# The router of a mixture of experts, merged into the stage of the shared expert

## What is computed

```python
g_s = silu(einsum('td,edf->etf', xf, Wg_s))
u_s = einsum('td,edf->etf', xf, Wu_s)
shared_out = einsum('etf,efd->td', g_s * u_s, Wd_s)      # F = 1536
logits = xf @ W_router + expert_bias                     # 625 x 8
top_vals, top_idx = jax.lax.top_k(logits, 2)
rw = softmax(top_vals, axis=-1)
...
routed_out = einsum('etd,te->td', out_e, combine)
x = x + shared_out + routed_out                          # xf is the layernorm of x
```

## Time and profile before

| what | us |
|---|---|
| device time, median of 3 runs | 2313.23 (2312.05 to 2313.57) |
| the profiled execution: its own time | 2312.01 |
| the profiled execution: span from its first to its last instruction | 2310.2 |
| PE, PEld, DVE, ACT, POOL busy | 2071.9, 1954.6, 1318.2, 888.6, 94.1 |
| the last four phases begin at about | 1450.6, 1469.6, 1520.0, 1718.2 |

### The profile page before, as it was taken

One profiled execution on the slowest core, in us unless ns is written; L12 is line 12 of the kernel. 1 busy time (PEld: TensorE's weight loads), 2 busy tenths in 40 slices (PEclk: granted clock), 3 DMA queues, 4 the chain that ended last, 5 costly groups with the idle time before them and its releaser, 6 DMA issues. The chain is left out here.

```text
span 2310.2 us, 34323 instructions
## 1 busy us (share of the span) xinstructions
PE 2071.9 (90%) x13804; PEld 1954.6 (85%) x13804; DVE 1318.2 (57%) x1912; ACT 888.6 (38%) x1078; POOL 94.1 (4%) x60
## 2 busy tenths in 40 slices
PE   5799889999999999945899979569989999999996
PEld 4788779999999999945899879569978888888885
DVE  9444376343344344355445546444238998889986
ACT  1233331221121121101355532122227777777775
POOL 0000000000000000000001000100001010100101
PEclk7999989999999999976899979679999999999998
DMA  2310026111212021110310030222229999999997
GB/s 64 98 42 28 1 77 164 49 49 33 65 49 64 28 76 53 45 28 0 103 28 28 1 130 15 95 82 98 88 76 383 387 386 379 374 370 379 370 371 278
DMA packets 186286, 313.74 MB, mean 136 GB/s; under 512 B 12769, under 2 KB 87012, under 8 KB 185756
## 3 DMA queue, kind: packets, MB, share of 16 engines
q1 hardware_dynamic: 178972, 294.53, 36.3%
q0 software_dynamic: 4816, 16.62, 3.1%
q10 hardware_dynamic: 2384, 0.92, 0.2%
HBM read 293.56 MB, written 20.40 MB: 136 GB/s over the span
## 5 line engine op out<-in xcount | busy, mean ns | idle before, releaser
L179 PE MATMUL psum<-re_whi,xt_sb 128*128 128x512 f32 (+1 forms) x1680 | 502.7, 374 | 1.5 <-DVE xt_sb L2706 1.5
L179 PE MATMUL psum<-ring_hi,xt_sb 128*128 128x256 f32 (+3 forms) x1980 | 369.8, 284 | 16.9 <-DVE a_sb L689 8.8
L179 PEld LDWEIGHTS psum<-re_whi,xt_sb 128*128 128x128 f32 x1680 | 312.7, 189 | 42.8 <-issue 1.9
L179 PEld LDWEIGHTS psum<-ring_hi,xt_sb 128*128 128x128 f32 (+1 forms) x1980 | 312.4, 190 | 18.4 <-DVE a_sb L689 9.6
L2690 DVE TENSOR_TENSOR re_wlo<-moe_raw,re_whi 128x1536 fp32r<-128x1536 f32 x173 | 303.4, 1756 | 34.2 <-ACT re_whi L2644 32.2
L179 PE MATMUL psum<-re_wlo,xt_sb 128*128 128x512 f32 (+1 forms) x840 | 311.6, 371 | 0.0
L2644 ACT ACTIVATE re_whi<-moe_raw 128x1536 fp32r<-128x1536 f32 x174 | 258.8, 1490 | 89.4 <-PE psum L179 86.4
L179 PE MATMUL psum<-ring_lo,xt_sb 128*128 128x256 f32 (+3 forms) x990 | 280.8, 284 | 0.0
L179 PEld LDWEIGHTS psum<-ring_lo,xt_sb 128*128 128x128 f32 (+1 forms) x990 | 188.2, 190 | 0.0
L179 PEld LDWEIGHTS psum<-re_wlo,xt_sb 128*128 128x128 f32 x840 | 158.8, 189 | 19.9
L128 ACT ACTIVATE ring_hi<-ring_raw 128x1536 fp32r<-128x1536 f32 (+2 forms) x67 | 102.3, 1526 | 175.8 <-PE psum L187 81.3
(11 more groups left out here) (386 smaller groups left out, 3322.3 us busy)
## 6 DMA issues: line engine op xcount, KB each, us to landing
moe_raw<-in_L_ffn_Wg_r SPq DMA_DIRECT2D x74, 768.0 KB, 9.5
moe_raw<-in_L_ffn_Wu_r SPq DMA_DIRECT2D x58, 768.0 KB, 8.7
moe_raw<-in_L_ffn_Wd_r SPq DMA_DIRECT2D x42, 768.0 KB, 7.0
re_more<-in_L_ffn_Wd_r SPq DMA_DIRECT2D x42, 768.0 KB, 9.6
re_more<-in_L_ffn_Wu_r SPq DMA_DIRECT2D x30, 768.0 KB, 8.2
ring_raw<-in_L_gnn_w_rel SPq DMA_DIRECT2D x18, 896.0 KB, 5.1
re_more<-in_L_ffn_Wg_r SPq DMA_DIRECT2D x15, 768.0 KB, 7.9
ring_raw<-in_L_mix_W_qkv SPq DMA_DIRECT2D x24, 384.0 KB, 4.4
```

Source lines behind the costliest of these rows:

```text
L179: mm = pe.matmul(out, lhs[a], rhs[b], start=(first and i == 0), stop=(last and i == 2))
```

## The change

`phase_router` and `phase_shared_expert` become one phase, `phase_router_shared`, so one barrier goes.

- `phase_norm` has an SP block. In the last norm SP loads the router's weights and the bias there, then the first three chunks of the shared expert. ACT makes the high part of the router's weights after the square root, DVE the low part after its last tile.
- The logits are made with the router's weights stationary (128 x 8) and the tokens streaming: 6 feature tiles x 3 x 2 halves = 36 matmuls of 314 columns onto 8 partitions. ACT adds the bias as it copies them out (`turned`), and PE turns them back in five small transposes between the gate and the up product of the first hidden tile.
- The rest of the router's work lies between tiles of the first half: ranks on PE after f = 1 (`RANK_AT`), DVE's `place()` behind it, DVE's `hold()` at f = 2, the tables after f = 4 (`TABLES_AT`).
- The shared expert has 3 split buffers where it had 4, so chunks 3 and 4 are split at f = 2, chunk 5 and the next half's first two at f = 5, and its third at the next half's f = 0. PSUM is used as three pairs in turn, the fourth belongs to the router. The down projection has six banks where it had four.
- SP writes `xn_dram` at the start of the merged phase, and ACT waits for it before its first silu. `later` shrinks from 128 x 3140 to 128 x 128.

```diff
-def phase_norm(k, name, keep=False):
+def phase_norm(k, name, keep=False, first_loads=None, router=None):
...
+            if router:
+                dve.wait_ge(s["router_hi"], 1)
+                dve.tensor_tensor(k.router_w[:, 1, :, :], k.router_f[:], k.router_w[:, 0, :, :].bitcast(F32), ALU.subtract)
...
-            for t in range(TT):
-                for j in range(KD):
-                    mm = split_product(pe, k.banks[0][0:TS[t], t * EXPERTS:(t + 1) * EXPERTS],
-                                       [k.xt[:, j, a, t * P:t * P + TS[t]] for a in range(2)],
-                                       [w[:, a, j, :] for a in range(2)], j == 0, j == KD - 1)
...
-    SPL = 4
+    SPL = 3
...
+            def logit_products():
+                for j in range(KD):
+                    mm = split_product_wide(pe, logit_pair, [k.router_w[:, a, j, :] for a in range(2)],
+                                            lambda b_, h: k.xt[:, j, b_, h * HN:(h + 1) * HN], j == 0, j == KD - 1)
+                mm.then_inc(s["logit_mm"], 1)
+
+            def turn_logits():
+                pe.wait_ge(s["logits_out"], 1)
+                for t in range(TT):
+                    mm = pe.transpose(router_bank[0:TS[t], t * EXPERTS:(t + 1) * EXPERTS], turned[:, t * P:t * P + TS[t]],
+                                      k.ident[0:EXPERTS, 0:EXPERTS])
+                mm.then_inc(s["mm"], 1)
...
+            logit_products()
+            for n in range(2):
+                for f in range(FT):
+                    gate_up(n, f)
+                    if n == 0 and f == RANK_AT:
+                        rank_products()
+                    if n == 0 and f == TABLES_AT:
+                        table_products()
+                down(n)
...
+            split_high(act, 0, 0)
+            split_high(act, 0, 1)
+            act.wait_ge(s["logit_mm"], 1)
+            act.activation(halves(turned[:]), logit_pair[:, :, 0:HN], ACT.Identity, bias=k.router_b[:, 0:1]).then_inc(s["logits_out"], 1)
+            split_high(act, 0, 2)
...
+            act.wait_ge(s["kept"], 16 * len(ROWS))
...
+                    if n == 0 and f == RANK_AT:
+                        place()
+                    if n == 0 and f == RANK_AT + 1:
+                        hold()
+                    if n == 0 and f == TABLES_AT:
+                        tables()
```

More of the change, by code:

```diff
@@ L2082, in phase_router @@
         empty = k.sb(f"{name}_empty", [P, JC], F32)
[L2083 to L2096, removed]
@@ new lines, in rank_products @@
+            def rank_products():
+                pe.wait_ge(s["later_made"], 2)
+                pe.wait_ge(s["sel_made"], 1)
+                for t in range(TT):
+                    for u in range(t + 1):
+                        pe.matmul(rank_bank[0:TS[t], t * EXPERTS:(t + 1) * EXPERTS],
+                                  (later if u == t else ones)[0:TS[u], 0:TS[t]],
+                                  selb[0:TS[u], u, :], start=(u == 0), stop=(u == t))
+                for u in range(TT):
+                    mm = pe.matmul(rank_bank[:, COUNTS:COUNTS + EXPERTS], ones[0:TS[u], :], selb[0:TS[u], u, :],
+                                   start=(u == 0), stop=(u == TT - 1))
+                mm.then_inc(s["rank_mm"], 1)
@@ L2361, in unit, with down @@
+            def down(n):
                 for c in range(2):
                     pe.wait_ge(s["lo_done"], n * CH + (5 + c))
[L2363 removed]
+                    wh = views(n, 4 + c)
                     for t in range(TT):
@@ L2406, in _ @@
         def _(act):
-            def unit(half, n, first):
-                if first:
-                    for i in range(3):
-                        split_high(act, n, i)
+            split_high(act, 0, 0)
[3 more added lines that the diff above has]
+            split_high(act, 0, 2)
+            act.wait_ge(s["gap_made"], 1)
@@ L2411, in unit @@
+            act.activation(ex[:], gap[:], ACT.Exp).then_inc(s["ex_made"], 1)
+            act.wait_ge(s["wt_made"], 1)
+            act.activation(wt_hl[:, 0, :, :], wt[:], ACT.Copy).then_inc(s["wt_hi"], 1)
+            act.wait_ge(s["kept"], 16 * len(ROWS))
+            for n in range(2):
                 for f in range(FT):
                     gate_ready(act, n, f)
-                    if not (first and f < 2):
+                    if not (n == 0 and f < 2):
                         act.wait_ge(s["hf"], n * FT + (f - 1))
-                    act.activation(halves(act_g[:, f % 2, :]), banks_of(half, f)[0][:, :, 0:HN], ACT.Silu).then_inc(s["silu"], 1)
+                    act.activation(halves(act_g[:, f % 2, :]), gate_pair(f)[:, :, 0:HN], ACT.Silu).then_inc(s["silu"], 1)
@@ new lines, in low @@
+            def low(n, f):
+                dve.wait_ge(s["h_hi"], n * FT + (f + 1))
+                dve.tensor_tensor(ht[:, f, 1, :], hf[:, f % 2, :], ht[:, f, 0, :].bitcast(F32),
+                                  ALU.subtract).then_inc(s["h_lo"], 1)
+            for i in range(2):
+                split_low(dve, 0, i)
+            dve.memset(logits[:], 0.0)
+            dve.memset(ones[:], 1.0)
+            dve.memset(rank[:], 0.0)
+            link(dve.memset(before[:], 0.0))
+            dve.wait_ge(s["iota_made"], 1)
@@ L2442, in unit @@
+            dve.tensor_copy(iota[:], iota_i[:])
+            dve.tensor_copy(token[:], token_i[:])
+            link(dve.tensor_copy(spare[:], spare_i[:]))
+            split_low(dve, 0, 2)
+            choose()
+            for n in range(2):
                 for f in range(FT):
```

446 lines of the change are left out of this document (206 added, 240 removed).

## The result

The changed kernel takes 2270.52 us (median of 4 runs, 2267.95 to 2272.92) where the kernel before took 2312.64 beside it (2308.93 to 2313.57): ratio 0.9821, 95% interval 0.9802 to 0.9839. That is 42.1 us less. The forecast was 2269.0 in a range of 2263 to 2277. The profiled execution took 2272.92, its span 2271.2.

What follows compares the result with a forecast made beforehand. PE bounds the shared stage, PE and DMA the routed; the gap between norm and shared products is a chain. -55.6 + 8.5 - 2.7 + 3.3 + 2.4 = -44.1 us from 2312.0 gives 2267.9, median 2269, range 2263 to 2277.

Steps and rivals of the forecast that it cites:

- gap before the logits: Between the norm's end and PE's first logit product: only a small DVE instruction (0.2 us) and the barrier (0.4), together 0.6.
- logits: 36 matmuls of 314 columns at the merged phase's start: 22 at the lower clock, 14 at the upper, 7.9 us.
- first gate product at the upper clock: Tile 0's gate product in the shared expert: if the logits raise the clock, 2.7 us of low matmuls go.
- turning, ranks, tables: Small products moved onto PE's path in the shared stage: 0.8 + 1.0 + 1.5 us, 3.3 (2.2 to 4.6).
- stalls from three buffers: Tile 3's up product waits 1.2 us for chunk 3's low part in each half: 2.4 us (0 to 5).
- Rival (a): At the logits: narrow products don't raise the clock; logits take 9.6 us, 4.4 more in all, 2273.5 us; chance 20%.
- the routed stage starts from the same six chunks loaded ahead ... at nothing: Start of the routed stage: the last two chunks, freed at tile 5, have a 63 us down projection to land; no cost.
- Rival (d): At the routed stage: it waits for the six chunks loaded ahead, 4.7 MB, 12.8 us, giving 2281.9 us; chance 3%.
- (c): Shared stage: DVE's router arithmetic is not covered, all 5.0 + 16.5 us fall on PE's path, 2290.6 us; chance 5%.
- (e): Shared stage: DVE becomes the bound, PE waiting at every tile, for splits and router work; +28.9, 2342 us; chance 3%.
- The slack of `hold()`: DVE's 10.7 us at f = 2 cost nothing: 3 us to spare for tile 3's multiplication, 2.5 for the tables.
- The early loads: Loads issued in the norm, 18.5 us ahead: the router's 4.5 us wait goes, first chunks at nothing, some 2 if slowed.

## Why the prediction came out right, and where it did not

The median came out 1.5 us above the forecast. The mechanism is the forecast one: the chain of 55.62 us left PE's path, and what took its place cost what was added up for it, within 1.8 us in all. That the total lies so close is in part luck, since this gain and a loss of 3.5 us in the routed stage cancel in part. By its own steps, in the profiled execution:

| term | forecast | measured |
|---|---|---|
| gap before the logits | 0.6 | 0.4 |
| logits | 7.9 | 7.0 (6.6 again) |
| first gate product at the upper clock | -2.7 | seen: 1.00 from 1478 |
| turning, ranks, tables | 3.3 | 0.4 + 0.76 + 1.12 = 2.3 |
| stalls from three buffers | 2.4 | 2 x 1.36 = 2.7 |
| stage without the norm | -44.1 | -45.9 |
| the norm itself | 0 | +1.3 |
| routed stage | 0 | +3.5 |
| before the last norm | 0 | +2.1 |

The turning is read from where PE's next group starts (1485.94 after 1485.50), the ranks and tables from the distance of two of DVE's multiplications (11.25 and 11.61 for 10.49), the stalls likewise (11.85 for 10.49; PE's idle time is 1.13 of each). The measured terms sum to 0.4 + 7.0 + 2.3 + 2.7 = 12.4 where the forecast had 14.2, and that is the 1.8 between -44.1 and -45.9.

**Rival (a), that the logits leave the clock low,** did not happen. Its premise is true all the same for narrow products: put into the changed kernel, they too read 0.50 for 18.91 us. Which of the two properties, 8 columns or 8 partitions, made the difference was open in the prediction; the experiments on the logits' form show for these shapes that the 8 partitions don't keep the clock down. The logits were 0.9 us shorter than forecast because the clock rose near 1477, after 16 of the 36, and not after 22 as in the shared stage before.

**What failed is the step "the routed stage starts from the same six chunks loaded ahead ... at nothing".** I asked there only for what the routed stage waits for, and its loads indeed cost nothing. I did not ask where its buffers lie. A few small tiles with a longer life, 580 bytes in all, moved them, which cost 0.2 us for each of 13 jobs, 2.6 to 2.7 of the 3.5; the rest lies at the stage's two ends, and the same edit took it away too (591.5 us). Rival (d) had a loss in the routed stage, but by late chunks, 12.8 us; no such wait appeared.

**The norm's +1.3** is the clock's: the transposes of the last norm ran at 0.50 in this trace, where the earlier trace rows has the last eighteen at 1.00. In the second trace of the same kernel the last eighteen ran at the upper clock (timeline of PE there, the first of its last groups and the logits):

```profile
1468.10 0.88 PE L226 MATMUL psum<-ident,a_sb 128*128 128x128 f32 x6 [1.33 <-DVE a_sb L287]
1474.60 6.72 PE L187 MATMUL psum<-xt_sb,router_w 128*8 128x314 f32 x36 [2.21 <-PEq L258]
```

The way from the norm's start to the first logit took 18.88 us there and 20.14 here: it comes out both ways with one code. So the two ends of the ranges given above are the changed kernel's two traces. Beside the one whose norm took as long, narrow logits cost 13.7 us, `hold()` done twice 9.1, and late loads 4.4, and four buffers gave 3.3. **The +2.1 ahead of it** lies in unchanged code. PE was busy at the lower clock for 114.7 us of that stretch in this trace and for 109.3 in the kernel before, which I estimate at 2.7 us, but no run tests it. That these were not in the range's working was harmless only because the small terms came out 1.8 us lower.

**Three readings were wrong where little hung on them.** The choice of experts was put at 5.0 us; the earlier trace rows have 3.9, from the end of the narrow logits (1495.08) to 1499.01, and the 5.0 holds the ranks' 1.0 a second time, so rivals (c) and (e) were priced 1 us too high. The 12.4 us of the earlier trace rows were taken for all three chunks. And the last chunks of the routed experts have no down projection of 63 us as cover but one half's, 31.6 by the prediction's own figure; they landed at 1654.0 and 1656.1, some 20 us before the routed stage began, so nothing waited for them.

**The slack of `hold()`** was the term most worth testing, since all the router's arithmetic was costed at nothing on it. It was 2.95 us, for an estimated 2.5 to 3. **The early loads** were a term hidden in the gap of 55.6. Their removal showed 4.4 to 6.1 us; the 11 of Theory 1 came from taking the landing time of the third transfer for that of the first.

## What to carry to other kernels

A chain of small dependent steps beside an engine that sets the length elsewhere is worth most of its length when moved (here 44.7 of 55.6 us), if each piece is costed by the slack of the engine it moves to; find the one piece with the least slack and test it by doubling it. This product with few output features was better made with the weights stationary and the tokens streaming, even with transposes behind it: 36 matmuls and five transposes took 8.7 us with their copy where 90 narrow ones took 19. A few small tiles left allocated can cost more than they look: the prediction had nothing for them. And after any change to what is allocated, compare a stage whose instructions did not change: if PE is busier for the same work, look at the addresses.

## What the runs showed of the hardware that I had not expected

- The same matmuls ran slower when 580 bytes of each partition stayed allocated ahead of their operands: 399 ns for 393 in the 512-column group, 341 as before in the 384-column one, 40.20 us for 40.00 per job. Back at the old place they ran as before.
- A PE that is busy by the profile for 18.91 us, with 90 matmuls of 8 columns, left the clock at 0.50. Under 36 matmuls of 314 columns onto only 8 partitions it rose to 1.00, in the changed kernel and in the kernel before.
- Sixteen products of the identity ahead of the norm, and a few behind each tile, kept the granted clock at 0.91 on average from the norm's start to the first logit, where it was 0.59 and 0.72 without them, at no cost in the norm's 18.5 us, and gave 1.3 to 3.0 us back.
- Three transfers of 1152 KB issued within 1 us landed 5.7, 9.8 and 12.3 us after their own issue: a time from issue to landing depends on the transfer's place among those issued with it.
